# Second expert stage: when finished rows may be gathered, six token tiles per five pairs

## The reference, cut to what matters

```python
def _L0_ffn_ref(x, router_w, w_gate, w_up, w_down):
    logits = xt @ router_w.T
    topk_vals, topk_idx = jax.lax.top_k(logits, TOP_K)      # TOP_K = 2 of 8 experts
    g = jax.nn.sigmoid(topk_vals)
    g = g / (g.sum(axis=-1, keepdims=True) + 1e-10)
    for e in range(E):
        ge = jnp.sum(jnp.where(topk_idx == e, g, jnp.zeros_like(g)), axis=-1)
        h = jax.nn.silu(xt @ w_gate[e]) * (xt @ w_up[e])
        out = out + ge[:, None] * (h @ w_down[e])
...
x = x + 0.5 * _L0_ffn_ref(_layernorm(x, axis=-1), ...)
x = x + _L0_attn_ref(_layernorm(x, axis=-1), ...)
x = x + 0.5 * _L0_ffn_ref(_layernorm(x, axis=-1), ...)
```

## Time and profile before

| | us |
|---|---|
| median of 3 runs | 1318.93 (1318.46 to 1321.54) |
| the profiled execution | 1321.73 |
| its span (first to last instruction) | 1320.0 |
| PE busy | 1078.9 (82%) |
| DVE busy | 901.4 (68%) |
| ACT busy | 768.8 (58%) |
| POOL busy | 540.9 (41%) |

### The profile page before, as it was taken

One profiled execution on the slowest core, in us unless ns is written; L12 is line 12 of the kernel. 1 busy time (PEld: TensorE's weight loads), 2 busy tenths in 40 slices (PEclk: granted clock), 3 DMA queues, 4 the chain that ended last, 5 costly groups with the idle time before them and its releaser, 6 DMA issues. The chain is left out here.

```text
span 1320.0 us, 23316 instructions
## 1 busy us (share of the span) xinstructions
PE 1078.9 (82%) x6351; PEld 898.4 (68%) x6351; DVE 901.4 (68%) x2699; ACT 768.8 (58%) x1987; POOL 540.9 (41%) x595
## 2 busy tenths in 40 slices
PE   3578989998988999989989878986858999898820
PEld 3467877877866777767767666764637878777720
DVE  7667677768634778786868677567856775777742
ACT  5345655545548786877777747765625665454510
POOL 3615445654023333332223235530630465555565
PEclk9979999999989999999989889997879999999965
DMA  8535354444240000000000000001232344444352
GB/s 263 168 118 196 118 167 141 146 139 133 67 159 21 17 19 18 19 15 15 17 13 17 13 21 33 28 21 41 96 144 61 98 120 124 115 116 114 105 159 74
DMA packets 134330, 114.41 MB, mean 87 GB/s; under 512 B 15424, under 2 KB 118336, under 8 KB 134080
## 3 DMA queue, kind: packets, MB, share of 16 engines
q1 hardware_dynamic: 108864, 64.71, 16.4%
q0 software_dynamic: 16384, 33.59, 8.6%
q10 hardware_dynamic: 8960, 14.63, 3.2%
HBM read 52.90 MB, written 59.97 MB: 86 GB/s over the span
## 5 line engine op out<-in xcount | busy, mean ns | idle before, releaser
L605 POOL DMA_INDIRECT x_dispatched<-xn_sb,row x256 | 250.5, 979 | 259.5 <-DVE row L569 110.4
L380 POOL DMA_INDIRECT f_y_in<-y_dispatched,row x160 | 151.3, 946 | 115.1 <-issue 56.0
L953 POOL TENSOR_TENSOR x_skip<-tok,d_skip 128x256 f32<-128x256 f32 x64 | 40.9, 640 | 318.3 <-DVE y L1385 174.0
L1002 PE MATMUL bank<-xT_high,wc_high 128*128 128x512 f32 x256 | 129.3, 505 | 3.8 <-DVE xT_low L1311 3.1
L380 POOL DMA_INDIRECT y_in<-y_dispatched,row x96 | 95.1, 991 | 37.3 <-issue 19.8
L1002 PE MATMUL bank<-xT_high,wc_low 128*128 128x512 f32 x256 | 104.1, 407 | 0.0
L1002 PE MATMUL bank<-xT_low,wc_high 128*128 128x512 f32 x256 | 104.1, 407 | 0.0
L770 DVE TENSOR_TENSOR f_hf<-f_sg,banks 128x512 f32<-128x512 f32 x84 | 56.3, 670 | 61.5 <-issue 30.5
L736 PE MATMUL bank<-shared,f_hh 128*128 x326 | 92.5, 359 | 0.1
L744 ACT ACTIVATE f_sg<-banks 128x512 f32<-128x512 f32 x84 | 49.1, 585 | 70.8 <-PE banks L716 56.9
L1370 DVE TENSOR_TENSOR state<-state_decayed,bank 128x256 f32<-128x256 f32 x56 | 23.6, 421 | 91.4 <-PE bank L1071 88.1
(11 more groups left out here) (281 smaller groups left out, 3370.6 us busy)
## 6 DMA issues: line engine op xcount, KB each, us to landing
f_xr<-x_dispatched SPq DMA_DIRECT2D x79, 128.0 KB
y_dispatched<-f_yr SPq DMA_DIRECT2D x79, 128.0 KB
e_xr<-x_dispatched SPq DMA_DIRECT2D x76, 128.0 KB
y_dispatched<-e_yr SPq DMA_DIRECT2D x76, 128.0 KB
w_split<-shared ACTq DMA_DIRECT2D x8, 768.0 KB
shared<-w_split SPq DMA_DIRECT2D x8, 768.0 KB
x_dispatched<-xn_sb,row POOLq DMA_INDIRECT x256
out_dram<-x_sb SPq DMA_DIRECT2D x8, 512.0 KB
```

Of the source, the lines that this page charges most:

```text
L380: nc.gpsimd.indirect_dma_start(out=self.y_in[n % 4][k][:], out_offset=None, in_=self.rows[t], in_offset=bass.IndirectOffsetOnAxis(ap=row[k ...
L605: nc.gpsimd.indirect_dma_start(out=xd_dram[g.x_home], in_=xn_sb[:, t, :], in_offset=None, out_offset=bass.IndirectOffsetOnAxis(ap=row[k][: ...
L1002: last = pe.matmul(acc[:], wc[w][:, tap, k * P:(k + 1) * P], xTb[x][:, at:at + 512], start=(tap == 0 and i == 0), stop=(tap == CONV_K - 1 ...
```

## The change

The table is filled with a step of 5/6 pair a tile in place of one pair, and rounded down. A group still starts no earlier than three pairs behind its last pair. And since a step of DVE's loop may now have two tiles, the lookup of one tile is a loop over the tiles. Nothing else is edited.

```diff
-            FETCH = []
+            PER_TILE = 5 / 6
+            at, FETCH = ALL_SENT, []
             for g in LAYER2:
+                at = max(at, g.pair_end + SETTLED)
                 for t in range(g.first, g.end):
-                    FETCH.append(max(g.pair_end + SETTLED, FETCH[-1] + 1 if FETCH else ALL_SENT))
+                    FETCH.append(int(at))
+                    at += PER_TILE
...
-                        if i - LANDING in FETCH:
-                            combine.dve(dve, FETCH.index(i - LANDING))
+                        for t in range(TILES):
+                            if FETCH[t] == i - LANDING:
+                                combine.dve(dve, t)
```

## The result

The changed kernel took 1337.65 us (median of 4 runs, 1333.04 to 1340.26) against 1319.19 us: a ratio of 1.0133, with a 95% interval of 1.0098 to 1.0168. It is slower by 1.3%, where 1313.2 us and a gain had been forecast, and it lies above the upper end of the range, 1324. The profiled execution took 1340.26 us, its span is 1338.5 us; before, they were 1321.73 and 1320.0, so the two executions differ by 18.5 us.

A forecast was written before the change was run, and what follows sets the result against it. The pairs' pace, slowed beside gathers, was taken to bound the kernel until PE ends, then POOL's gathers of the remaining tiles. Terms of -10.0, +1.4 and +2.9 summed to -5.7 us, giving 1313.2 us, range 1307 to 1324.

The forecast's parts named there:

- (a): Tail behind the last pairs: four tiles fewer left to gather at 2.50 us each, -10.0 us.
- (c): Loop over pairs: eight steps combining two tiles lengthen gather runs, 0.36 us each, +2.9 us, upper end 14.6.
- (b): Loop over pairs: four more tiles gathered beside the pairs at 0.36 us a tile, +1.4 us.
- Rival 4: Loop over pairs: runs of six gathers hold PE 1.82 us more at each of eight two-tile steps; 1324.9 us, chance 0.18.
- Rival 1: Loop over pairs: PE's late completions don't come from the gathers' density, so the loop pays nothing; 1308.9 us, chance 0.20.
- Rival 3: Gathers: the ring of four buffers sets the pace, 3.37 us a tile, eating the saving; 1322.4 us, chance 0.15.

The follow-up runs named there:

- e15: The changed kernel, unedited, measured again on chip 6: 1262.4 us against 1269.3 for the kernel before, ratio 0.9935.
- e7: The kernel before with two extra 128x128 additions on DVE in eight steps, on chip 5: 1267.6 us, ratio 0.9981.
- e12: The kernel before with two extra 128x128 additions on DVE in eight steps, on chip 3: 1269.2 us, ratio 1.0010.
- e2: The kernel before with eight pairs of buffers, two tiles released together at every second pair, on chip 0: 1325.5 us, ratio 1.0037.
- e3: The kernel before with eight pairs of buffers, four tiles released together at every fourth pair, on chip 0: 1381.2 us, ratio 1.0458.
- e1: The kernel before with eight pairs of buffers in place of four in the last stage, one tile a pair, on chip 0: 1306.1 us, ratio 0.9871.
- e4: The kernel before with all gathers of the last stage moved behind the loop over pairs, on chip 0: 1421.7 us, one run.
- e9: The changed kernel, unedited, measured again on chip 0: 1348.0 us against 1333.5 for the kernel before, ratio 1.0132.
- e10: The changed kernel with eight pairs of buffers in place of four in the last stage, on chip 0: 1334.0 us, ratio 0.9992 to the kernel before.
- e17: The kernel before with eight pairs of buffers, each tile's second gather also waiting for a down, on chip 7: 1319.0 us, ratio 0.9886.
- e18: The changed kernel with eight pairs of buffers and 11 tiles per ten pairs, on chip 7: 1327.7 us, ratio 0.9955 to the kernel before.
- e5: The changed kernel with eight pairs of buffers in place of four in the last stage, on chip 5: 1258.7 us, ratio 0.9910 to the kernel before.
- e6: The changed kernel with plain DMAs in place of the last stage's gathers, on chip 5: 1247.1 us, ratio 0.9812 to the kernel before.
- e11: The changed kernel with plain DMAs in place of the last stage's gathers, on chip 0: 1285.0 us, ratio 0.9632 to the kernel before.

## Why the prediction was wrong

**What bounds the kernel** was read rightly, and so was the tail. Step (a) gave -10.0 and the trace shows -7.5, with the mechanism that it named (tile 49 in the place of tile 45) and 3.6 us more of long waits behind it; in e15, where nothing is late, it is the full amount (52.0 us from pair 79 to the end, against 60.9 and 63.3 in e7 and e12, which have the tail of before).

**The step that failed is (c)**, with (b): together +4.3 us, with 14.6 as the upper end of (c), and measured +26.2. Two things were wrong in it. First, the price of a longer run came from one run of six in the trace of before, by the distance of two combines (5.74 against 3.92 and 5.38, so 0.36 to 1.82 us). The last completion that a run holds comes behind the run's end, so a run that is 2.5 us longer can hold it for 2.5 us more: e2's runs of four cost 24.8 us over 22 runs, 1.1 us each, e3's of eight 7.8 us each ((80.3 - 2 x 1.1)/10). The right size stood in the earlier trace rows: silu 4.07 us idle beside six gathers of the first stage, 3.0 more than in an undisturbed step; in the changed kernel silus come 3.4 to 3.7 us late beside three of the sixes. The prediction set it against the 1.12 us beside four of the earlier trace rows, which is hardly more than the 1.06 of an undisturbed step, though that silu was 1.5 us late: idle time and lateness were taken for the same. The count of a run, six behind a double step, was right for eight of the ten long runs; the other two went on to eight and ten, since the sixth gather can end after the following tile is released. Rival 4 was played down with "the run ends by itself": so it does, but only when the stall has begun, at six or eight gathers. Second, the clock: the forecast took PE's matmuls at the level of the earlier trace rows throughout, but behind long stalls it fell, 9.8 of the 26.2 us.

There was a sum to be made that would have warned, from numbers that the prediction had: twelve gathers at 1.25 us are 15.0 us, and five undisturbed pairs 14.9. The table asked for all of POOL's time, so that the pauses, with which the loss had been 18.5 us, had to shrink wherever the pairs kept their pace. A single run of four or six is the wrong thing to price when the change takes away the gaps between runs.

**Rival 4** was right in kind and its threshold was passed: it decides at 1.08 us a double step, and (26.2 - 1.4)/8 is 3.1. Its price, 1.82, was too small for the same reason. **Rival 1** (the loop pays nothing, 1308.9) is what happens on chips 3, 5 and 6, to the extent that POOL keeps up. The Trainium skill, SBUF — State Buffer, on its two separate sides, has it that a DMA and a compute instruction can't slow each other and that TensorE and ScalarE wait for nobody at the ports of SBUF. The traces agree on either kind of chip: the silu at 1176.94 takes 0.60 us, as an undisturbed one does. But the page says nothing of when a completion is passed on, and that is what is late on chips 0 and 7 (6.3 us), so the prediction drew more from it than it states when it made (b) and (c) nothing by it. **Rival 3** (the ring sets the pace) is nearly e15: on a chip where nothing else is late DVE waits for rows in the loop, which the prediction had named as the sign that (a) is wrong. In the trace of the result DVE doesn't, and completions are late, so there it is rival 4 and not rival 3.

The undisturbed pace was taken as 2.98 us a pair, 134.1 for the stretch; it is 131.7, so the kernel before lost 18.5 us there and not 16.2.

## What to carry to other kernels

Before a helper engine is asked for a higher rate beside a pipeline, add up what share of its time the rate takes: at 100% no pauses are left but those that the disturbance itself makes, and its work joins into long runs. And where a trace shows a wait that nothing in it explains, measure on more than one chip: the same change was 1.3% slower in two measurements and 0.7% faster in a third, on a chip of another kind.

## What the runs showed of the hardware

- On chips 0 and 7 indirect DMAs issued by GpSimd one behind the other make the engines that wait for TensorE get its completions late, while TensorE itself goes on with what it has: 1.5 us late beside four, 6.3 beside eight. Not every completion is late. Over the traces of this kind (the result's two, e1 to e4, e9, e10, e17 and e18), in runs of four gathers and more, 12 of the 102 that fell into a run's first 1.9 us and found ScalarE idle were over 0.1 us late, and 140 of the 148 that fell later than 3.1 us into it. The last one held comes the later the longer the run was: by the median 0.7 us behind the end of a run of two, 1.1 behind four, 1.5 behind six, 1.7 behind eight, 1.9 behind the one of ten.
- On chips 3, 5 and 6, 36 in a row delay nothing (0.04 us, e5). What sets the two kinds apart isn't known.
- Plain DMAs from the same engine, as many and as large, in runs of up to four (2.5 us), delay nothing on either kind (e6, e11), and take 0.53 us each in place of 0.94.
- Stalls cost twice: behind stretches of 2.5 to 5.5 us without a matmul the granted clock was at its lower level (0.50) for some 3 to 7 us (0.50 from 1121.8 to 1125.1 and from 1155.9 to 1162.7), behind seven of the eight such stretches of the changed kernel. PE's matmuls took 9.8 us longer by it.
